# Opening units of an attention and feed-forward layer: zero products ahead of the data, v of unit 0 by weight blocks, GpSimd's work reordered, slab 1 inside unit 2's step

## The reference, cut to what matters

```
q, k, v = x @ Wq.T + bq, x @ Wk.T + bk, x @ Wv.T + bv      # 16 heads of 32
q, k = rope(q), rope(k)
qk  = einsum('bshd,bstd->bsht', q, k) / sqrt(32)           # heads against heads, for each token
att = softmax(qk)
x   = layernorm(x + einsum('bsht,bstd->bshd', att, v) (heads and tokens swapped) @ Wo.T + bo)
g, u = (x @ gate_w.T) * gate_s, (x @ up_w.T) * up_s        # 1408 wide
x   = layernorm(x + ((silu(g) * u) @ down_w.T) * down_s)
```

## Time and profile before

| | us |
|---|---|
| median of 3 runs (range) | 1680.69 (1678.19 to 1681.34) |
| the profiled execution's own time | 1678.94 |
| its span, first to last instruction | 1677.2 |
| TensorE busy | 1650.0 |
| VectorE busy | 1316.7 |
| ScalarE busy | 981.9 |
| GpSimd busy | 630.6 |

### The profile page before, as it was taken

The page is one execution under the profiler, slowest core; times in us unless marked ns, Lnnn a source line. Parts: engine busy times, 40 slices in busy tenths (PEclk is TensorE's granted clock), DMA queues, the critical chain, the costliest instruction groups (busy, mean ns, idle before and its releaser), DMA issues.

```text
span 1677.2 us, 40834 instructions
## 1 busy us (share of the span) xinstructions
PE 1650.0 (98%) x14958; PEld 1354.0 (81%) x14958; DVE 1316.7 (79%) x1932; ACT 981.9 (59%) x1578; POOL 630.6 (38%) x690
## 2 busy tenths in 40 slices
PE   8899999999999999999999999999999999999997
PEld 6688888888888888886888888888888888888886
DVE  7889999999999999998667676676766666767656
ACT  5666666666666666666454554655645545556453
POOL 7767666676667666643101102011011020110112
PEclk9999999999999999999999999999999999999999
DMA  6677878787777878778744535525445364353351
GB/s 211 153 185 169 186 169 196 173 175 177 184 188 167 189 169 194 175 168 257 246 141 138 164 104 170 164 93 189 153 141 161 101 197 159 103 191 119 113 181 59
DMA packets 438708, 275.53 MB, mean 164 GB/s; under 512 B 257280, under 2 KB 377216, under 8 KB 438656
## 3 DMA queue, kind: packets, MB, share of 16 engines
q1 hardware_dynamic: 438512, 274.61, 60.2%
q10 hardware_dynamic: 144, 0.26, 0.0%
HBM read 181.74 MB, written 93.06 MB: 164 GB/s over the span
## 4 chain that ended last, share of the span: by engine, by line
PE 92%; DVE 2%; SPq 2%; issue 1%; ACT 1%; POOL 1%; DMA 1%; POOLq 0%; DVEq 0%; ACTq 0%
PE ps_x L646 12%; PE ps_x L650 12%; PE ps_x L647 12%; PE ps_s L918 9%; PE ps_s L923 9%; PE ps_x L918 8%; PE ps_x L923 7%; PE ps_x L929 5%; PE ps_x L933 5%; PE ps_s L791 3%; PE ps_a L778 2%; PE ps_a L929 2%; PE ps_a L933 2%; PE ps_s L929 2%; PE ps_s L933 2%
## 5 line engine op out<-in xcount | busy, mean ns | idle before, releaser
L918 PE MATMUL ps_s<-x_hi,slot 128*128 128x512 f32 x672 | 264.6, 394 | 0.4
L923 PE MATMUL ps_s<-x_lo,slot 128*128 128x512 f32 x672 | 262.2, 390 | 0.0
L1531 POOL TENSOR_TENSOR z<-z,xr 128x512 f32<-128x512 f32 x60 | 77.0, 1307 | 480.5 <-DVE z L1907 480.5
L918 PE MATMUL ps_x<-x_hi,slot 128*128 128x512 f32 x560 | 219.5, 392 | 3.5 <-ACT sg L1246 1.9
L923 PE MATMUL ps_x<-x_lo,slot 128*128 128x512 f32 x560 | 218.5, 390 | 0.0
L1101 ACT ACTIVATE kX<-kT 32x512 f32<-32x512 f32 x256 | 161.2, 630 | 63.1 <-DVE kT L1640 45.0
L1841 DVE TENSOR_TENSOR hid<-ps_s,hid 128x512 f32<-128x512 f32 x88 | 60.8, 691 | 122.8 <-ACT hid L1254 122.8
L918 PEld LDWEIGHTS ps_s<-x_hi,slot 128*128 128x128 f32 x672 | 126.4, 188 | 34.8 <-ACT u L1285 4.3
L923 PEld LDWEIGHTS ps_s<-x_lo,slot 128*128 128x128 f32 x672 | 126.4, 188 | 25.3
L929 PE MATMUL ps_x<-wd,h 128*128 128x512 f32 x352 | 137.1, 390 | 0.2 <-DVE h L1882 0.2
L933 PE MATMUL ps_x<-wd,h 128*128 128x512 f32 x352 | 137.0, 389 | 0.0
(11 more groups left out here) (178 smaller groups left out, 4398.9 us busy)
## 6 DMA issues: line engine op xcount, KB each, us to landing
slot<-gu_hi SPq DMA_DIRECT2D x88, 896.0 KB, 5.1
xc<-x_cols SPq DMA_DIRECT2D x32, 512.0 KB, 3.8
v_rows<-v_in SPq DMA_DIRECT2D x32, 512.0 KB, 2.8
v<-v_rows SPq DMA_DIRECT2D x32, 512.0 KB, 5.2
res<-x_rows SPq DMA_DIRECT2D x64, 256.0 KB, 3.8
x_rows<-x_out SPq DMA_DIRECT2D x32, 512.0 KB, 3.8
x_cols<-x_turn SPq DMA_DIRECT2D x128, 128.0 KB, 2.5
raw<-x_cols SPq DMA_DIRECT2D x64, 256.0 KB, 5.1
```

Of the source, the lines that this page charges most:

```text
L918: pe.matmul(out[:, :], slot[:, WEIGHTS[i], cols], x_hi[:, i, k], start=start, stop=False, skip_group_check=True)
L923: last = pe.matmul(out[:, :], slot[:, WEIGHTS[i], cols], x_lo[:, i, k], start=False, stop=stop, skip_group_check=True)
L1531: pool.tensor_tensor(z[:, h, r], z[:, h, r], rows_of_x1(n, h)[:, r], ALU.add).then_inc(z_added[h], 1)
```

## The change

It makes six edits, all in the opening and in step 2. (1) POOL zeroes `warm`, 128 x 128 numbers in the buffer of the probabilities, and TensorE multiplies it by itself ten times before its first product. (2) x of unit 0 is loaded in two DMAs, a tile each, with a semaphore each. (3) v of unit 0 goes over the weight blocks outside and the two tiles inside, with a wait for each operand just ahead of the pass that needs it. (4) POOL's opening has a new order: splits of x of unit 1 first, then weight sums Q5 and Q6, x of unit 2 and its sums, weight sum Q7, and later the rest. ACT's and DVE's openings follow it; Q4's weights are split late (on DVE inside step 2). (5) POOL's sums of slab 1 are at the end of the opening. (6) `high_of_slab(1)` on ACT and `low_of_slab(1)` on POOL move out of the opening into step 2: on ACT behind `exponent(1)`, on POOL behind `s_lo` of Q6 of unit 3 and ahead of the sums of slab 2; `top_of_slab(1)` comes two instructions later. SP's order is unchanged but for (2).

```
+            def first_v():
+                for k in range(KE):
+                    for t in range(2):
+                        out = ps_x[BANK_Y if t else BANK_W][:, :]
+                        if t == 0:
+                            pe.wait_ge(wv_hi_done, k + 1)
+                        pe.wait_ge(a_hi_done, t + 1)
+                        pe.matmul(out, a_hi[:, t, k], wv_hi[:, k], start=k == 0, stop=False, skip_group_check=True)
+                        pe.wait_ge(wv_lo_done, k + 1)
+                        pe.matmul(out, a_hi[:, t, k], wv_lo[:, k], start=False, stop=False, skip_group_check=True)
+                        pe.wait_ge(a_lo_first, t + 1)
+                        last = pe.matmul(out, a_lo[:, t, k], wv_hi[:, k], start=False, stop=k == KE - 1, skip_group_check=True)
...
-            project_v(0, 0)
-            project_v(0, 1)
+            pe.wait_ge(power_set, 1)
+            for _ in range(WARM):
+                pe.matmul(ps_x[BANK_X][:, 0:P], warm, warm, start=True, stop=True)
+            first_v()
...  ACT, step
                 exponent(u - 1)
                 if second:
-                    top_of_slab(u - 1)
+                    high_of_slab(u - 1)
                 high_of_tile(u + 1, 0)
                 high_of_sum(u + 1, Q6)
-                if not second:
+                if second:
+                    top_of_slab(u - 1)
+                else:
                     normalise_x1(u - 3)
                 high_of_slab(u)
...  ACT, opening
-            high_of_block(Q5)
             high_of_tile(1, 0)
             high_of_tile(1, 1)
             spread_k(0, 0)
+            high_of_block(Q5)
+            spread_k(0, 1)
+            high_of_tile(2, 0)
+            high_of_tile(2, 1)
             high_of_block(Q6)
-            spread_k(0, 1)
             for k in range(KE):
                 high_of_wo(k)
             high_of_block(Q7)
-            high_of_block(Q4)
+            exponent(0)
             high_of_slab(0)
-            exponent(0)
-            high_of_tile(2, 0)
-            high_of_tile(2, 1)
             spread_k(1, 0)
-            top_of_slab(0)
             spread_p(0)
+            high_of_sum(2, Q6)
             spread_k(1, 1)
-            high_of_sum(2, Q6)
             high_of_sum(2, Q7)
             high_of_sum(2, Q5)
-            high_of_slab(1)
+            high_of_block(Q4)
+            top_of_slab(0)
...  POOL, step
                     low_of_tile(u + 1, 0)
                     low_of_sum(u + 1, Q6)
+                if isinstance(u, int) and u == DIRECT:
+                    low_of_slab(u - 1)
                 sums_of_slab(u)
...  POOL, opening
+            low_of_tile(1, 0)
+            low_of_tile(1, 1)
             sum_of_weights(Q5)
             sum_of_weights(Q6)
-            low_of_tile(1, 0)
-            low_of_tile(1, 1)
+            low_of_tile(2, 0)
+            low_of_tile(2, 1)
+            sums_of_tiles(2)
             sum_of_weights(Q7)
-            sum_of_weights(Q4)
             sums_of_slab(0)
             for k in range(KE):
                 low_of_wo(k)
+            sum_of_weights(Q4)
             low_of_slab(0)
-            sums_of_tiles(2)
-            low_of_tile(2, 0)
-            low_of_tile(2, 1)
-            sums_of_slab(1)
             low_of_sum(2, Q6)
             low_of_sum(2, Q7)
             low_of_sum(2, Q5)
-            low_of_slab(1)
+            sums_of_slab(1)
...  DVE, step 2, ahead of subtract_top(1)
                 low_of_heads(u - 2)
+                if not later:
+                    low_of_block(Q4)
                 subtract_top(u - 1)
```

More of the change, by code:

```diff
@@ L37 @@
 OPENING = 4
+WARM = 10
 DIRECT = 2
@@ L132, in post_ln_layer @@
             prob = sb("prob", [P, 2 * Q32, H], F32, early)
+            warm = prob[:, 0:8].rearrange("p n k -> p (n k)")
             with ExitStack() as staged:
@@ L219, in post_ln_layer @@
         xc_loaded, xc1_loaded = sem("xc_loaded"), sem("xc1_loaded")
+        x0_loaded = [xc_loaded, sem("x0_second_loaded")]
         res_loaded = [sem(f"res_loaded{t}") for t in range(2)]
@@ L379, in _ @@
             load_weight(WV, 0)
-            sp.dma_start(x_view(xc), x_cols2[0]).then_inc(xc_loaded, 16)
+            for t in range(2):
+                sp.dma_start(x_view(xc)[:, t], x_cols2[0, :, t]).then_inc(x0_loaded[t], 16)
             for k in range(1, KE):
@@ L729, in project_v @@
                 for k in range(KE):
-                    if isinstance(m, int) and m == 0:
-                        pe.wait_ge(wv_hi_done, k + 1)
-                        pe.wait_ge(wv_lo_done, k + 1)
                     last = three(ps_x[bank][:, :], hi[:, t, k], lo[:, t, k], wv_hi[:, k], wv_lo[:, k],
@@ L735, in project_v @@
                 last.then_inc(v_done, 1)
+            def first_v():
+                for k in range(KE):
+                    for t in range(2):
+                        out = ps_x[BANK_Y if t else BANK_W][:, :]
[7 more added lines that the diff above has]
+                        last = pe.matmul(out, a_lo[:, t, k], wv_hi[:, k], start=False, stop=k == KE - 1, skip_group_check=True)
+                        if k == KE - 1:
+                            last.then_inc(v_done, 1)
             def project_heads(m, t):
@@ L1074, in high_of_tile @@
                 elif isinstance(m, int) and m == 0:
-                    act.wait_ge(xc_loaded, 16)
+                    act.wait_ge(x0_loaded[t], 16)
                 else:
@@ L1323, in super_step @@
                         copy_s1(0, 0)
-                        act.wait_ge(power_set, 3)
+                        act.wait_ge(power_set, 4)
                         act.activation(table[:, :], ones[:, :], ACT.Silu)
@@ L1406, in sum_of_weights @@
                 pool.tensor_tensor(B_RAW[q], a, b, ALU.subtract).then_inc(w_summed, 1)
+            pool.memset(warm, 0.0).then_inc(power_set, 1)
             pool.memset(power[:, :], -0.5).then_inc(power_set, 1)
@@ L1411, in _ @@
             pool.memset(kX[:, :, :, :, :], 0.0).then_inc(kX_zeroed, 1)
-            pool.wait_ge(power_set, 3)
+            pool.wait_ge(power_set, 4)
             def low_of_wo(k):
@@ L1803, in _ @@
             turn_k(0, 0)
-            low_of_block(Q5)
             plain_k(0, 1)
-            turn_k(0, 1)
             plain_q(0, 0)
             turn_q(0, 0)
+            turn_k(0, 1)
             plain_q(0, 1)
             turn_q(0, 1)
+            low_of_block(Q5)
+            add_v_bias(1, 0)
             low_of_block(Q6)
-            add_v_bias(1, 0)
+            add_v_bias(1, 1)
             dve.wait_ge(late_loaded, 16 * 3)
@@ L1816, in _ @@
             subtract_top(0)
-            low_of_block(Q7)
-            add_v_bias(1, 1)
-            sums_of_prob(0)
             plain_k(1, 0)
             turn_k(1, 0)
+            sums_of_prob(0)
             scale_prob(0)
             plain_k(1, 1)
-            turn_prob(0)
             plain_q(1, 0)
             turn_q(1, 0)
+            turn_prob(0)
+            plain_q(1, 1)
             turn_k(1, 1)
-            plain_q(1, 1)
             turn_q(1, 1)
-            low_of_block(Q4)
+            low_of_block(Q7)
             rest_of_step(DIRECT)
```

## The result

| us | before | after |
|---|---|---|
| median | 1680.42 (1678.19 to 1681.34, 4 runs) | 1693.68 (1691.85 to 1694.64, 4 runs) |
| the profiled execution's own time | 1678.94 | 1693.88 |
| its span | 1677.2 | 1692.1 |

What follows compares the result with a forecast made beforehand. TensorE bounds the kernel, held in step 3 by a chain from f_lo of slab 1. 11.1 - 0.3 + 1.6 = +12.4 on 1678.94 gives 1691.3, or 1693.1 by the median; forecast 1692, range 1684.5 to 1695.

Steps and rivals of the forecast that it cites:

- The slab chain: f_lo of slab 1 through slab 2's load to TensorE's last Q2 product in step 3: +11.1 us, chance 0.72.
- the lower bound: Store of slab 1 to landing of slab 2: shorter issues could take 3.8 less; none of it was taken.
- The signs: Trace after, step 3: ACT waits over 10 us for slab 2's sums, TensorE stands 11 to 12 for kX.
- The opening: Edits 1 to 5: start gains 2.5 us, 2.2 given back before exponent(1); first data product 5.9, Q7 wait 1 to 3.
- the -0.3: The opening's net effect on exponent(1), ahead of f_lo of slab 1: 0.3 us earlier.
- The new order: Slab 1's sums at the end of GpSimd's opening wait for a load behind f_lo of slab 0: up to +1 us.
- The clock: Behind TensorE's stand of almost 12 us in step 3, products 0.43 apart for some 3 us: +1.6, other end 0.
- The issue wait: TensorE's 3.64 us on issue amid the scores, loop's first pass: unchanged, ends 3.6 less and 0.5 more.
- The profiled execution and the median: Forecast summed on the profiled execution's 1678.94; the median of the runs shown was taken as 1.75 above it.
- The shorter bill: Rival: opening's whole gain arrives, issue wait vanishes or clock stays up; +3.4 to +9 us, chance 0.13.
- the three reliefs: Opening's whole gain reaching the exponential (-3.0), issue wait vanishing in the long stand (-3.6), clock staying up (-1.6).
- The other side: Rival: TensorE's start is gained and kept, 1675.5 if all 5.2 came through; needs slab 2 by 62; chance 0.08.

Runs made afterwards that it cites:

- the start alone: Edits 1 to 3 on the kernel before: 1682.80 (ratio 1.0010); again with x of unit 0 in one DMA (edits 1 and 3): 1681.67 (ratio 1.0002).
- the start over slab 1 early: Kernel before with slab 1's store and split earlier, VectorE's low parts of Q7 and Q4 later, and edits 1 to 3: 1680.12 (ratio 0.9999).
- slab 1 early: Kernel before with slab 0 stored right behind slab 1's load, f_hi of slab 1 behind spread_p(0), f_lo right behind its sums: 1680.81 (ratio 1.0003).
- filled kernel: Changed kernel with 36 useless products of 512 columns on TensorE ahead of Q1 of step 3, during its long stand: 1691.65 (ratio 1.0068).
- half of edit 6: Changed kernel with, in step 2, f_hi of slab 1 ahead of exponent(1) and f_lo of slab 1 ahead of the output bias: 1689.07 (ratio 1.0047).

## Why the prediction was right, point by point

**The slab chain (predicted +11.1, less 0.3 of the opening; measured +10.9).** Each station came within 0.9 of the forecast. `f_lo` of slab 1 ended at 67.2, for 66.4: the output bias started at 59.84 instead of 58.98, after a wait for the residual's load, which had no term. Slab 2 landed at 76.34, for about 76: store to landing took 9.2, not 10.1, so a part of the lower bound (issues that get shorter) did come. TensorE passed at 84.93, for about 85. The two errors, 0.8 and 0.9, cancel by luck. The residual was late because its load is issued behind the stores of slab 0, at 54.55 instead of 47.64: that much of the new order's cost is on the path in the changed kernel too. The kernel with edit 6 alone shows the whole mechanism without the rest.

**The signs.** ScalarE waited 9.76 for the sums of slab 2, not over 10, and TensorE stood 9.2, not 11 to 12. It came to the last product of Q2 2.2 later than in the kernel before, held up by the stand before Q7 and by the products at 0.43 behind it, which the forecast had not carried that far.

**The opening (predicted: 2.5 won at the start, given back before `exponent(1)`).** The first data product came at 6.12 (5.9), v of unit 0 ended at 12.1 (11.8), the new stand before Q7 was 1.8 (1 to 3). The ten products of zeroes took 4.63, to 5.63 instead of 5.3, still ahead of the data. With GpSimd idle until 17.75, VectorE's splits at 14.26 and 16.00 took 1.23 and 1.22, where the same two took 2.55 and 2.83 before. `exponent(1)` ran at 58.93, 0.5 later than in the earlier trace rows, where 0.3 earlier was forecast: given back and a little more. It wasn't what held `f_lo` of slab 1, though: `f_hi` of slab 1 was done at 60.75, and GpSimd came to `f_lo` at 65.24 without a pause from the output bias on. So the -0.3 stood for a path that didn't bind. The kernels with the start alone and with the start over slab 1 early show that it also gains nothing where the slab isn't moved; VectorE takes it by 28 us.

**The new order (predicted: no cost of its own, up to +1 by slab 1's load): right for a wrong reason.** The sum priced the new order by its effect on `exponent(1)` alone and left out the one buffer of `f_hi`. The kernel without edit 6 shows what the order does: `f_lo` of slab 0 9.5 us later, its store later, and `f_hi` of slab 1 stopped for 5.10 on it, with heads, evictions and 8.1 us of TensorE behind. In the changed kernel edit 6 hides all of that cost but the 0.9 of the residual. The forecast therefore holds for the whole change, and the attribution to edit 6 is right for that edit on the kernel before; but the -0.3 for the other edits holds at best beside edit 6. Without it they cost 9.3.

**The clock (predicted +1.6; measured +3.6).** This term of the sum was mis-sized. I priced one fall of the clock, by the eight products at the start of the earlier trace rows, and took it for granted that it stays up behind the issue wait, because there it had stayed up before. In the changed kernel it is down before the issue wait, reads 0.98 in the 2 us ahead of the resumed scores, and is at 0.50 again for 92 to 98. The filled kernel separates the two: 2.0 won back where the stand is filled, the later stretch slow all the same, if shorter (products 0.43 apart until 94.4 instead of 98.4). (The Trainium skill, TensorE: Matmul & The Clock Gate, "What's actually happening", has the throttled state as the default. These traces agree with it as to the long stand; the 3.64 of the earlier trace rows, which cost no clock, stands beside 3.98 in the filled kernel, which did.)

**The issue wait (predicted unchanged, ends -3.6 and +0.5; measured +0.5).** Right in size. But it isn't a constant: it varies from 1.6 to 5.3 with the DMA traffic beside it.

**The profiled execution and the median.** By the trace the change costs 14.9, by the medians 13.3: the profiled execution of before lay 1.5 below its median, the one of after 0.2 above.

**The rivals.** The shorter bill would have needed one of the three reliefs; none came, and all three terms went the other way (0.5 later for 0.3 earlier, an issue wait of 4.15 for 3.64, 3.6 for 1.6 of the clock). The other side needed slab 2 to land by 62; it landed at 76. Nothing of the opening's gain came through in any kernel by itself, even with slab 1 early, which the rival took for its condition (`f_lo` of slab 1 by 52; it ended by 50.7 with the start on top). There TensorE passed Q2 at 73.16, 0.9 earlier than before, and the issue wait and the clock behind it took that back.

## What to carry to other kernels

A second stream with one buffer for each stage binds through its whole ring (load, sums, split, store), so an instruction of it that moves must be followed to the next load and, for each buffer, to the store that frees it; too late at either end cost 9 to 11 us here. When a chain is taken off the path and nothing is gained, look for a wait that no engine releases, and for what the DMA queues carry while it lasts: one wait on the issuing queue was worth more (3 to 6 us) than the whole rearrangement of the opening. Gains at the start of TensorE are worth nothing while another engine, here VectorE, takes them back before the steady part.

## What the runs showed of the hardware that was not expected

- The size of a wait in front of no releaser depends on other traffic: 3.5 to 5.3 us with slab stores and loads under way (a DMA share of 1.20 in the kernel before), 1.6 to 2.5 with the DMA engines nearly idle (0.08 to 0.19), at the same place in the scores.
- Products came 0.43 apart behind stands of 1.8, 4.8, 8.1, 9.2 and 10.0 us, behind ten of the eleven issue waits of 3.5 to 5.3 and behind the one of 2.54. They did not behind the 3.64 of the kernel before, nor behind 2.41, 1.98 and 1.61. The same stand of 1.78 before Q7 was followed by 0.43 in the changed kernel (61.31 to 64.30) and by 0.23 in the filled one, which is the same program up to there. The length of a stand alone doesn't tell.
- The 20 records of zero products, 4.63 us, were followed by data products 0.23 to 0.39 apart in six of the eight traces that have them (leaving out the first distance, which can hold a wait), and 0.43 apart in the other two.
- A ScalarE instruction that waited 5.10 for a DMA store had "issue" as its releaser in the profile: a wait for a landing can look like a wait for nothing. With half of edit 6 the same instruction stood 1.21 on "issue", until 58.05, and the store that it waited for, issued at 52.23, took 5.7 to land.
